# Graph layer with expert gates: gates kept in 32 partitions per tile of nodes, bias products of two tiles at a time, tiles in the order 0, 2, 1, 3

## The chip, the cores and the metric

One NeuronCore of a Trainium2 chip runs the whole program. The metric is the device time of one execution in microseconds, as the median of several runs. The engines are TensorE (PE in the rows, its weight loads PEld), VectorE (DVE), ScalarE (ACT), GpSimd (POOL) and SyncE (SP), which here only issues DMAs.

## What is computed

The reference is one layer over 12,500 nodes of 256 channels: a normalisation, a graph attention term and a linear attention term (phase 1 and the first half of phase 2 of the kernel), and then a feed-forward part with one shared and four gated expert networks. Only the last of these matters here:

```python
def _shared_mlp(x, W1, b1, W2, b2, W3, b3):
    h = jax.nn.relu(x @ W1 + b1)
    h = jax.nn.relu(h @ W2 + b2)
    return h @ W3 + b3
...
all_out = _experts_mlp(x, eW1, eb1, eW2, eb2, eW3, eb3)      # 4 experts, 256 -> 128 -> 64 -> 256
shared = _shared_mlp(x, sW1, sb1, sW2, sb2, sW3, sb3)         # 256 -> 256 -> 128 -> 256
gates = jax.nn.softmax(x @ gW + gb, axis=-1)
topv, topi = jax.lax.top_k(gates, TOPK)                       # the best 2 of 4
topw = jax.nn.softmax(topv, axis=-1)
sel = jnp.take_along_axis(all_out, topi[:, :, None, :], axis=-1)
gated = jnp.sum(sel * topw[:, :, None, :], axis=-1)
return shared + gated
```

Since the experts' last layer is linear, the kernel multiplies the hidden activations by the gates before the last weights, and adds the last biases as one more product: a row of up to 32 numbers for each node (its four gates as high part, low part and high part again, and two ones for the shared bias) times a matrix of 32 rows and 256 columns.

## The kernel before

The nodes are worked on in 25 groups of 500, a group being 4 tiles of 125 nodes (`T = 4`, `R = 125`). Phase 1 (to about 255 us) makes the tables that the graph term gathers from, and phase 2 (from about 255 us) is a software pipeline whose turn `i` does three stages: `a` for group `i`, `b` for group `i-1` and `c`, the feed-forward part, for group `i-2`. Turns 2 to 24 have all three stages, so there are 23 such turns; the groups 23 and 24 get their feed-forward part in `last_turn` and `end_turn`.

Each engine's instructions are written out by hand in program order, and engines wait for one another only by named semaphores. Nothing is reordered by a scheduler. The products are in fp32r, a rounded 32-bit form; one product with full accuracy is three of them (`split_mm`, L228 to L230: high by high, low by high, high by low).

The gates travel so. VectorE writes a group's gates into `scale_rows` (125 x 128: 32 numbers for each of the 4 tiles). TensorE transposes that (L606) into psum partitions 0 to 127, tile `j` in partitions 32j to 32j+31. ScalarE's `copy_scales` (L958 to L963) moves the four blocks of 32 partitions to `scaleT`, all of them to partitions 0 to 31, tile `j` in columns 125j to 125j+124. The other 96 partitions of `scaleT` and of `out_bias` hold zeros for good. `scaleT` is then read twice: by L691, which spreads the gates over the experts' channels with the selection matrix `gate_sel`, and at the end of the turn by L706, the bias product of each tile, `scaleT` (128 x 125) as weights and `out_bias` (128 x 256) streamed.

The last part of TensorE's turn is this, for each of the tiles 0, 1, 2, 3: one bias product, three products of the shared last layer, and six of the experts' last layer, all added up in one half of a psum bank (tiles 0 and 1 in bank 2, tiles 2 and 3 in bank 3). It waits for `e2_lo` (the low part of the gated activations, made by VectorE) ahead of tile 0's expert products. Its end is told by `out_mm`, for which VectorE's last addition of the turn waits. In `last_turn` and `end_turn` the same products stand in `out_shared` (bias and shared layer of four tiles, each tile in a bank of its own) and `out_experts`.

Two other places run TensorE in narrow form: `p2_den` (L507) and `logits_of_z` (L613) multiply 128 rows by only 32 columns of weights, four of them side by side, to psum partitions 0, 32, 64 and 96; they are plain fp32 products and show two records for each. `second_experts` (L595) does the same with 64 columns.

`small_constants` on VectorE builds `gate_sel`, `out_bias` and others once, near 234 to 240 us.

Of the kernel before, what the change touches and what calls it, by code (L numbers as in the profile page):

```python
# [8 lines left out]
ALU = mybir.AluOpType  # L9
ACT = mybir.ActivationFunctionType  # L10
# [3 lines left out]
C = 256  # L14
HEADS, HEAD_CH = 4, 64
MIX_HEADS, MIX_CH = 8, 32
EXPERTS, TOPK = 4, 2
LN_EPS, ATT_EPS = 1e-5, 1e-6

P = 128  # L20
R = 125
T = 4
# [7 lines left out]
QUAD = 32  # L30
# [6 lines left out]
for _name, _chunks, _cols in (("Wq", 2, 256), ("W1", 4, 512), ("W2", 4, 256), ("sW1", 2, 256), ("sW2", 2, 128),  # L37
# [2 lines left out]
    W_TOTAL += _chunks * _cols  # L40

SEMAPHORES = (
    "base", "den", "den_rows", "dx", "e1_mm", "e1_relu", "e2_hi", "e2_lo", "e2_mm", "e2_relu", "e2g",
    "g_hi", "g_split", "gate_rows", "gates", "gath0", "gath1", "gb", "gnn", "gw", "h_lo", "h_mm", "h_relu", "hb_mm", "ident", "lg", "lg_mm", "lt_mm",
    "idx0", "idx1", "k_exp", "kden", "k_hi", "k_mm", "k_split", "kf", "kvT", "kv_mm", "kx", "kxT", "kxs", "kxt_mm", "mT",
    "mT_hi", "m_mm", "m_norm", "masks", "mt", "mv_m", "mv_x1", "mv_y", "mv_z", "out", "out_mm", "p1_act",
# [9 lines left out]
def gps_layer(nc, A):  # L56

    ctx = ExitStack()
    with ctx:
# [5 lines left out]
        def due(count):  # L65

            return not isinstance(count, int) or count > 0
# [144 lines left out]
        def rowt(b, j):  # L212

            return psum[0:R, b + j // 2, (j % 2) * C:(j % 2 + 1) * C]
# [4 lines left out]
        def wslice(t, name, chunk, lo=0, n=None):  # L219
            at, cols = W_AT[name]  # L220
            at += chunk * cols + lo
            return t[:, at:at + (cols if n is None else n)]

        def split_mm(pe, out, w, x, first, last):


            (wh, wl), (xh, xl) = w, x
            pe.matmul(out, wh, xh, start=first, stop=False)  # L228
            pe.matmul(out, wh, xl, start=False, stop=False)  # L229
            return pe.matmul(out, wl, xh, start=False, stop=last)  # L230
# [195 lines left out]
        def _(pe):  # L426
# [11 lines left out]
            def tile(t, c, j):  # L438
                return t[:, c, j * R:(j + 1) * R]
# [134 lines left out]
            def w2_pair(i, pair, c):  # L574
# [12 lines left out]
                                        (wslice(w_hi, "W2", k), wslice(w_lo, "W2", k)), k == 0, k == 3)  # L587
                last.then_inc(S["w2"], 1)

            def second_experts(i, q):  # L590

                pe.wait_ge(S["e1_relu"], 4 * (i - 2) + 2 * q + 2)
                for m in range(2):
                    e = 2 * q + m
                    last = pe.matmul(psum[m * HEAD_CH:(m + 1) * HEAD_CH, 2 + q, 0:GR], second_w[:, e, :], e1[:, e, :],  # L595
                                     start=True, stop=True)
                last.then_inc(S["e2_mm"], 1)

            def phase2(i, par, a=True, b=True, c=True, own_q=True):
# [99 lines left out]
                if c:  # L699
                    if due(i - 1):  # L700
                        pe.wait_ge(S["s2_lo"], i - 1)
                    if due(2 * (i - 1)):
                        pe.wait_ge(S["e2_relu"], 2 * (i - 1))
                    for j in range(T):
                        out = rowt(2, j)
                        pe.matmul(out, scaleT[:, j * R:(j + 1) * R], out_bias[:], start=True, stop=False)  # L706
                        split_mm(pe, out, (s2_hi[:, j * R:(j + 1) * R], s2_lo[:, j * R:(j + 1) * R]),
                                 (wslice(w_hi, "sW3", 0), wslice(w_lo, "sW3", 0)), False, False)
                        if j == 0:
                            if due(i - 1):  # L710
                                pe.wait_ge(S["e2_lo"], i - 1)
                        for q in range(2):
                            last = split_mm(pe, out, (tile(h_hi, q, j), tile(h_lo, q, j)),
                                            (wslice(w_hi, "eW3", q), wslice(w_lo, "eW3", q)), False, q == 1)
                    last.then_inc(S["out_mm"], 1)

            def expert(e, bank):
# [32 lines left out]
            def out_shared(i, banks, lows):  # L750

                pe.wait_ge(S["t_s2"], lows)
                pe.wait_ge(S["e2_relu"], 2 * (i - 1))
                for j in range(T):
                    pe.matmul(psum[0:R, banks[j], 0:C], scaleT[:, j * R:(j + 1) * R], out_bias[:], start=True, stop=False)
                    split_mm(pe, psum[0:R, banks[j], 0:C], (s2_hi[:, j * R:(j + 1) * R], s2_lo[:, j * R:(j + 1) * R]),
                             (wslice(w_hi, "sW3", 0), wslice(w_lo, "sW3", 0)), False, False)

# [117 lines left out]
        def _(act):  # L876
# [81 lines left out]
            def copy_scales(i):  # L958
                if due(i - 1):
                    act.wait_ge(S["scale_t"], i - 1)  # L960
                for j in range(T):
                    last = act.activation(scaleT[0:QUAD, j * R:(j + 1) * R], psum[j * QUAD:(j + 1) * QUAD, 5, 0:R],  # L962
                                          ACT.Copy)  # L963
                last.then_inc(S["scaleT"], 1)

            def expert(i, e, bank):
# [201 lines left out]
        def _(dve):  # L1168
# [71 lines left out]
            def small_constants():  # L1240
                dve.memset(head_mask[:], 0.0)
                dve.drain()
                for h in range(P // MIX_CH):
                    dve.memset(head_mask[h * MIX_CH:(h + 1) * MIX_CH, h * MIX_CH:(h + 1) * MIX_CH], 1.0)
                dve.wait_ge(S["w_later"], 16 * LATER_LOADS)
                for e in range(EXPERTS):
                    hi, lo = PARTS[0] + e, PARTS[1] + e
                    tt(gate_sel[:, e // 2, e % 2 * HEAD_CH:(e % 2 + 1) * HEAD_CH],
                       ident[:, hi:hi + 1].broadcast_to([P, HEAD_CH]),
                       ident[:, lo:lo + 1].broadcast_to([P, HEAD_CH]), ALU.add)  # L1250
                dve.reduce_sum(low_rows[:, 0:QUAD], ident[:].rearrange("p (j r) -> p r j", r=QUAD), AXX)
                dve.reduce_sum(third[:], ident[:, PARTS[2]:PARTS[2] + 8], AXX)
                dve.tensor_copy(ob_hi[0:QUAD, :], ob_raw[0:QUAD, :])
                dve.wait_ge(S["zeroed"], 1)
                dve.tensor_copy(gate_w[:, :, 0:EXPERTS], gw_raw[:])
                dve.drain()
                ts(third[:], third[:], -1.0, None, ALU.mult)
                dve.reduce_sum(w2_nmean[:], w2, AXX)
                for q in range(CK):
                    at = [d + q * per for d in (0, MIX_HEADS)]  # L1260
                    tt(den_sel[:, q, :].rearrange("p (h n) -> p h n", h=per),
                       low_rows[:, at[0]:at[0] + per].unsqueeze(2).broadcast_to([P, per, MIX_CH]),
                       low_rows[:, at[1]:at[1] + per].unsqueeze(2).broadcast_to([P, per, MIX_CH]), ALU.add)
                dve.reduce_sum(low_rows[:, QUAD:QUAD + 1], low_rows[:, MIX_HEADS:2 * MIX_HEADS], AXX)
                dve.drain()
                ts(low_rows[:, QUAD:QUAD + 1], low_rows[:, QUAD:QUAD + 1], -1.0, None, ALU.mult)
                ts(w2_nmean[:], w2_nmean[:], -1.0 / C, None, ALU.mult).then_inc(S["w2_mean"], 1)
                stt(out_bias[0:QUAD, :], ob_hi[0:QUAD, :], third[0:QUAD, :], ob_raw[0:QUAD, :], ALU.mult, ALU.add)

            def second_parts(n):  # L1270

# [595 lines left out]
```

## Time and profile before

| | |
|---|---|
| median of 3 runs | 1368.28 us (1367.68 to 1369.21) |
| the profiled execution, its own time | 1367.16 us |
| its span, first to last instruction | 1365.4 us |
| TensorE busy | 1324.2 us, 97% of the span |
| VectorE, GpSimd, ScalarE busy | 1034.3, 826.1, 738.2 us |
| granted TensorE clock, mean | 0.995 |
| one turn of phase 2 | 43.0 us |

The span leaves out 1.8 us of the execution around it. A row of the timeline gives the start and length of an instruction, or of several alike. A matmul's length includes its passage through the array, so neighbours overlap: what one costs in a stream is the distance from its start to the next one's start.

### The profile page before, as it was taken

To read this page: it belongs to the slowest core of one execution; us is meant where nothing else is said; L and a number is where in the kernel's file an instruction comes from. 1 tells how busy PE (TensorE), PEld (TensorE's weight loads), DVE (VectorE), ACT (ScalarE), POOL (GpSimd) and SP (SyncE) were. 2 spreads that over 40 slices of the span, in tenths; PEclk is the share of its full clock that TensorE was granted. 3 is DMA by queue.
4 is the path that set the end of the run, shared out by engine and by line. 5 is a ranking of instruction groups with operands and counts; after the bars stand their busy time and mean duration, and the time that the engine had idled before them with its cause. 6 is when DMAs were issued, how large, how long until landed. Compare 5 with 4: busy or idle time off the path is not lost.

```text
span 1365.4 us, 26647 instructions
## 1 busy us (share of the span) xinstructions
PE 1324.2 (97%) x8932; PEld 1149.0 (84%) x8932; DVE 1034.3 (76%) x2615; ACT 738.2 (54%) x1339; POOL 826.1 (61%) x818
## 2 busy tenths in 40 slices
PE   5999999988999999999999999999999999999997
PEld 5999999876888888888888888888888888888886
DVE  6877677977787777877778777877778777787774
ACT  4555555334655655556554555545565455655554
POOL 4777676757555675556655666556665566655540
PEclk9999999999999999999999999999999999999999
DMA  5787767422211221112211222122221222211001
GB/s 172 253 267 244 241 209 254 130 60 68 63 39 54 76 75 46 52 55 76 72 41 58 57 76 71 29 70 58 76 68 31 68 61 76 68 31 60 17 16 31
DMA packets 71736, 121.81 MB, mean 89 GB/s; under 512 B 38034, under 2 KB 42767, under 8 KB 71704
## 3 DMA queue, kind: packets, MB, share of 16 engines
q1 hardware_dynamic: 55704, 108.00, 24.8%
q0 software_dynamic: 16000, 13.43, 4.5%
q8 instruction: 14, 0.23, 0.1%
q14 instruction: 18, 0.15, 0.0%
HBM read 69.47 MB, written 51.70 MB: 89 GB/s over the span
## 4 chain that ended last, share of the span: by engine, by line
PE 86%; DVE 5%; ACT 3%; issue 3%; POOL 2%; POOLq 1%; DMA 1%; DVEq 1%; SPq 0%; ACTq 0%
PE psum L228 26%; PE psum L229 25%; PE psum L230 25%; PE psum L434 5%; DVE qf L1473 2%; PE psum L691 1%; ACT s_hi L956 1%; PE psum L613 1%; PE psum L507 1%; PE psum L514 1%; ACT relu L955 1%; PE psum L706 1%; POOL xg L1753 1%; POOL ag L1755 1%; DMA attn_bc<-in_L_gnn_attn_l 0%
## 5 line engine op out<-in xcount | busy, mean ns | idle before, releaser
L1759 POOL TENSOR_TENSOR s_lo<-relu,s_hi 128x1000 fp32r<-128x1000 f32 (+1 forms) x47 | 85.4, 1816 | 148.9 <-ACT s_hi L956 143.4
L228 PE MATMUL psum<-w_hi,h_hi 128*125 128x256 f32 x600 | 171.1, 285 | 0.1
L229 PE MATMUL psum<-w_lo,h_hi 128*125 128x256 f32 x600 | 168.8, 281 | 0.0
L230 PE MATMUL psum<-w_hi,h_lo 128*125 128x256 f32 x600 | 168.6, 281 | 0.0
L1759 POOL TENSOR_TENSOR h_lo<-relu,h_hi 128x1000 fp32r<-128x1000 f32 x50 | 124.6, 2492 | 50.6 <-ACT h_hi L956 50.5
L1753 POOL DMA_INDIRECT xg<-table_xt,idx x100 | 124.9, 1249 | 39.5 <-issue 38.3
L1755 POOL DMA_INDIRECT ag<-table_al,idx x100 | 122.4, 1224 | 30.5 <-issue 30.5
L228 PE MATMUL psum<-z_hi,w_hi 128*128 128x500 f32 x300 | 121.5, 405 | 1.8 <-DVE z_lo L1543 1.0
L228 PE MATMUL psum<-xT_hi,w_hi 128*128 128x500 f32 x300 | 120.2, 401 | 0.0
L229 PE MATMUL psum<-xT_lo,w_hi 128*128 128x500 f32 x300 | 117.7, 392 | 0.0
L230 PE MATMUL psum<-xT_hi,w_lo 128*128 128x500 f32 x300 | 117.1, 390 | 0.0
L229 PE MATMUL psum<-z_lo,w_hi 128*128 128x500 f32 x300 | 116.7, 389 | 0.0
L230 PE MATMUL psum<-z_hi,w_lo 128*128 128x500 f32 x300 | 116.7, 389 | 0.0
L228 PEld LDWEIGHTS psum<-w_hi,h_hi 128*125 128x125 f32 x600 | 111.8, 186 | 5.1 <-issue 4.4
L880 ACT ACTIVATE row_n<-psum,nm_m,rs_m 125x256 f32<-125x256 f32 x100 | 48.2, 563 | 123.5 <-POOL nm_m L1696 123.5
L229 PEld LDWEIGHTS psum<-w_lo,h_hi 128*125 128x125 f32 x600 | 111.8, 186 | 0.0
L230 PEld LDWEIGHTS psum<-w_hi,h_lo 128*125 128x125 f32 x600 | 111.5, 186 | 0.0
L1415 DVE SCALAR_TENSOR_TENSOR base<-xb,rn,b_bc 125x256 f32<-125x256 f32 x100 | 93.7, 977 | 0.0
L962 ACT ACTIVATE scaleT<-psum 32x125 fp32r<-32x125 f32 x100 | 26.7, 267 | 120.5 <-PE psum L606 119.6
L1284 DVE TENSOR_SCALAR qf<-psum 128x1000 f32<-128x1000 f32 x25 | 30.0, 1199 | 78.2 <-PE psum L230 78.0
L1729 POOL TENSOR_TENSOR k_lo<-kf,k_hi 125x1024 fp32r<-125x1024 f32 x25 | 63.3, 2532 | 41.7 <-DVE k_hi L1227 41.7
L968 ACT ACTIVATE e<-psum,e_bias 128x500 f32<-128x500 f32 x100 | 65.0, 672 | 35.9 <-PE psum L230 35.9
(264 smaller groups left out, 4343.4 us busy)
## 6 DMA issues: line engine op xcount, KB each, us to landing
xb<-in_x SPq DMA_DIRECT2D x50, 448.0 KB
xT_hi_table<-x1T_hi SPq DMA_DIRECT2D x25, 500.0 KB
xT_lo_table<-x1T_lo SPq DMA_DIRECT2D x25, 500.0 KB
xT_hi<-xT_hi_table SPq DMA_DIRECT2D x25, 500.0 KB, 4.3
xT_lo<-xT_lo_table SPq DMA_DIRECT2D x25, 500.0 KB, 5.4
table_xt<-xts SPq DMA_DIRECT2D x25, 455.0 KB
out<-xmid SPq DMA_DIRECT2D x24, 448.0 KB
xb<-in_x SPq DMA_DIRECT2D x50, 52.0 KB
```

The lines of the kernel that those rows point to most:

```text
L228: pe.matmul(out, wh, xh, start=first, stop=False)
L229: pe.matmul(out, wh, xl, start=False, stop=False)
L230: return pe.matmul(out, wl, xh, start=False, stop=last)
L434: last = pe.transpose(psum[:, b + c, j * R:(j + 1) * R], src[:, j, c * P:(c + 1) * P], ident[0:R, 0:R])
L880: act.activation(out[:, j, :], src(j), ACT.Identity, bias=nm[which][:, j:j + 1], scale=rs[which][:, j:j + 1]).then_inc(S[done], 1)
L968: act.activation(e1[:, e, :], colT(bank), ACT.Relu, bias=e1_bias[:, e:e + 1]).then_inc(S["e1_relu"], 1)
L1284: ts(qf[:], colT(bank, 2), 0.0, None, ALU.min).then_inc(S["q_min"], 1)
L1415: last = stt(base[:, j, :], xb[par][:, j, :], rn2[par][:, 0, j:j + 1], b2_bc[:], ALU.mult, ALU.add)
L1729: ptt(k_lo[par][:], kf[par][:], k_hi[par][:], ALU.subtract).then_inc(S["k_split"], 1)
L1753: pool.indirect_dma_start(xg[par][:, j, :], None, table_xt.ap(), bass.IndirectOffsetOnAxis(idx[par][:, 1, j:j + 1], 0)).then_inc(S[f"gath{ ...
L1755: pool.indirect_dma_start(ag[par][:, j, :], None, table_al.ap(), bass.IndirectOffsetOnAxis(idx[par][:, 0, j:j + 1], 0)).then_inc(S[f"gath{ ...
L1759: ptt(out, src, hi, ALU.subtract).then_inc(S[done], 1)
```

## The change

The gates of tile `j` stay in partitions 32j to 32j+31 on their way into `scaleT`, which so becomes block-diagonal (zeros elsewhere, as before). `out_bias` gets four copies of its 32 rows, one for each block of partitions, by three more VectorE copies, and `gate_sel` picks a gate from any of the four blocks (`low_rows` is the identity folded over the four blocks). A bias product now reads only its tile's 32 rows of `scaleT` and of `out_bias`. In the turn the tiles go in two pairs, 0 and 2, then 1 and 3, so that the two bias products of a pair write two banks. In each pair come two bias products, six products of the shared layer and twelve of the experts' layer. The wait for `e2_lo` stands behind the first pair's shared products, and a new semaphore, `first_out`, is raised by the last of these and waited for ahead of the second pair's bias products; both are on TensorE. In `out_shared` the four bias products stand together ahead of the four tiles' shared products.

```diff
+            def bias_of_gates(out, j):
+
+                part = slice(j * QUAD, (j + 1) * QUAD)
+                pe.matmul(out, scaleT[part, j * R:(j + 1) * R], out_bias[part, :], start=True, stop=False)
...
-                    for j in range(T):
-                        out = rowt(2, j)
-                        pe.matmul(out, scaleT[:, j * R:(j + 1) * R], out_bias[:], start=True, stop=False)
-                        split_mm(pe, out, (s2_hi[:, j * R:(j + 1) * R], s2_lo[:, j * R:(j + 1) * R]),
-                                 (wslice(w_hi, "sW3", 0), wslice(w_lo, "sW3", 0)), False, False)
-                        if j == 0:
-                            if due(i - 1):
-                                pe.wait_ge(S["e2_lo"], i - 1)
-                        for q in range(2):
-                            last = split_mm(pe, out, (tile(h_hi, q, j), tile(h_lo, q, j)),
-                                            (wslice(w_hi, "eW3", q), wslice(w_lo, "eW3", q)), False, q == 1)
+                    for second in range(2):
+                        if second:
+                            pe.wait_ge(S["first_out"], i - 1)
+                        for j in (second, second + 2):
+                            bias_of_gates(rowt(2, j), j)
+                        for j in (second, second + 2):
+                            last = split_mm(pe, rowt(2, j), (s2_hi[:, j * R:(j + 1) * R], s2_lo[:, j * R:(j + 1) * R]),
+                                            (wslice(w_hi, "sW3", 0), wslice(w_lo, "sW3", 0)), False, False)
+                        if second == 0:
+                            last.then_inc(S["first_out"], 1)
+                            pe.wait_ge(S["e2_lo"], i - 1)
+                        for j in (second, second + 2):
+                            for q in range(2):
+                                last = split_mm(pe, rowt(2, j), (tile(h_hi, q, j), tile(h_lo, q, j)),
+                                                (wslice(w_hi, "eW3", q), wslice(w_lo, "eW3", q)), False, q == 1)
                     last.then_inc(S["out_mm"], 1)
...
                 for j in range(T):
-                    pe.matmul(psum[0:R, banks[j], 0:C], scaleT[:, j * R:(j + 1) * R], out_bias[:], start=True, stop=False)
+                    bias_of_gates(psum[0:R, banks[j], 0:C], j)
+                for j in range(T):
                     split_mm(pe, psum[0:R, banks[j], 0:C], (s2_hi[:, j * R:(j + 1) * R], s2_lo[:, j * R:(j + 1) * R]),
...
                 for j in range(T):
-                    last = act.activation(scaleT[0:QUAD, j * R:(j + 1) * R], psum[j * QUAD:(j + 1) * QUAD, 5, 0:R],
-                                          ACT.Copy)
+                    part = slice(j * QUAD, (j + 1) * QUAD)
+                    last = act.activation(scaleT[part, j * R:(j + 1) * R], psum[part, 5, 0:R], ACT.Copy)
...
+                for e in range(EXPERTS):
+                    hi, lo = PARTS[0] + e, PARTS[1] + e
+                    tt(gate_sel[:, e // 2, e % 2 * HEAD_CH:(e % 2 + 1) * HEAD_CH],
+                       low_rows[:, hi:hi + 1].broadcast_to([P, HEAD_CH]),
+                       low_rows[:, lo:lo + 1].broadcast_to([P, HEAD_CH]), ALU.add)
...
+                dve.drain()
+                for j in range(1, T):
+                    dve.tensor_copy(out_bias[j * QUAD:(j + 1) * QUAD, :], out_bias[0:QUAD, :])
```

On TensorE, at the end of a turn, the kernel before has this order (operands are named as the moving operand, then the weights: `out_bias,scaleT` is a bias product, `w,s` the shared layer, `w,h` the experts' layer):

```order
L706 MATMUL psum<-out_bias,scaleT 125x256 [waits s_e2_relu,s_s2_lo]
L228 MATMUL psum<-w_hi,s_hi 125x256
L229 MATMUL psum<-w_lo,s_hi 125x256
L230 MATMUL psum<-w_hi,s_lo 125x256
L228 MATMUL psum<-w_hi,h_hi 125x256 [waits s_e2_lo]
L229 MATMUL psum<-w_lo,h_hi 125x256
L230 MATMUL psum<-w_hi,h_lo 125x256
L228 MATMUL psum<-w_hi,h_hi 125x256
L229 MATMUL psum<-w_lo,h_hi 125x256
L230 MATMUL psum<-w_hi,h_lo 125x256
L706 MATMUL psum<-out_bias,scaleT 125x256
```

The changed kernel has at the same place, from the beginning of the first pair to the wait for `e2_lo`:

```order
L593 MATMUL psum<-out_bias,scaleT 125x256 [waits s_e2_relu,s_s2_lo]
L593 MATMUL psum<-out_bias,scaleT 125x256
L228 MATMUL psum<-w_hi,s_hi 125x256
L229 MATMUL psum<-w_lo,s_hi 125x256
L230 MATMUL psum<-w_hi,s_lo 125x256
L228 MATMUL psum<-w_hi,s_hi 125x256
L229 MATMUL psum<-w_lo,s_hi 125x256
L230 MATMUL psum<-w_hi,s_lo 125x256
L228 MATMUL psum<-w_hi,h_hi 125x256 [waits s_e2_lo]
```

The number of products is the same; bias products now stand in twos, and eight products rather than four stand ahead of the wait for `e2_lo`.

In `last_turn` on TensorE the bias products stood one ahead of each tile's three shared products:

```order
L755 MATMUL psum<-out_bias,scaleT 125x256 [waits s_e2_relu,s_t_s2]
L228 MATMUL psum<-w_hi,s_hi 125x256
L229 MATMUL psum<-w_lo,s_hi 125x256
L230 MATMUL psum<-w_hi,s_lo 125x256
L755 MATMUL psum<-out_bias,scaleT 125x256
```

Now the four stand together:

```order
L593 MATMUL psum<-out_bias,scaleT 125x256 [waits s_e2_relu,s_t_s2]
L593 MATMUL psum<-out_bias,scaleT 125x256 x3
L228 MATMUL psum<-w_hi,s_hi 125x256
L229 MATMUL psum<-w_lo,s_hi 125x256
L230 MATMUL psum<-w_hi,s_lo 125x256
```

Here too only the order and the rows that a bias product reads have changed.

## Rows read from the trace of the kernel before

**Rows 1.** The page: busy time and share of each engine; clock by slices.
```profile
PE 1324.2 (97%) x8932; PEld 1149.0 (84%) x8932; DVE 1034.3 (76%) x2615; ACT 738.2 (54%) x1339; POOL 826.1 (61%) x818
...
PEclk9999999999999999999999999999999999999999
```
**Rows 2.** The page: the chain that ended last, by engine.
```profile
PE 86%; DVE 5%; ACT 3%; issue 3%; POOL 2%; POOLq 1%; DMA 1%; DVEq 1%; SPq 0%; ACTq 0%
```
**Rows 3.** Two turns of phase 2: span, then busy us of PE, PEld, DVE, ACT, POOL, clock.
```profile
643.11:686.18 43.07, 42.89 (x278) 36.12 (x277) 33.20 (x90) 23.80 (x43) 26.29 (x25) 1.00 0.21 60
686.18:729.20 43.02, 42.85 (x277) 36.08 (x277) 33.05 (x90) 23.93 (x44) 26.38 (x25) 1.00 0.21 60
```
**Rows 4.** Waits of PE over the whole span: us in total, times, longest.
```profile
PE psum L691 <- ACT s_hi L956: 3.8, 22, 0.2
PE psum L434 <- ACT row_n L880: 2.6, 1, 2.6
PE psum L755 <- DVE s_lo L1539: 2.1, 1, 2.1
```
**Rows 5.** Timeline of PE and PEld at the end of a turn (start, length).
```profile
695.86 0.38 PE L230 MATMUL psum<-xT_hi,w_lo 128*128 128x500 f32 x1
695.86 0.18 PEld L706 LDWEIGHTS psum<-out_bias,scaleT 128*125 128x125 f32 x1
696.08 0.28 PE L706 MATMUL psum<-out_bias,scaleT 128*125 128x256 f32 x1
...
696.20 0.28 PE L228 MATMUL psum<-w_hi,s_hi 128*125 128x256 f32 x1
...
697.26 0.28 PE L706 MATMUL psum<-out_bias,scaleT 128*125 128x256 f32 x1
```
**Rows 6.** Groups by line: the bias products of turns 2 to 24.
```profile
L706 PE MATMUL psum<-out_bias,scaleT 128*125 128x256 f32 x92 | 26.0, 282 | 0.0
```
**Rows 7.** Timeline around L507: 128 rows by 32 columns, four side by side.
```profile
679.04 0.38 PE L229 MATMUL psum<-z_lo,w_hi 128*128 128x500 f32 x1
...
679.26 0.38 PE L230 MATMUL psum<-z_hi,w_lo 128*128 128x500 f32 x1
679.58 0.37 PEld L507 LDWEIGHTS psum<-qf,kden 128*32 128x32 f32 x16 [0.34 <-issue]
679.58 0.64 PE L507 MATMUL psum<-qf,kden 128*32 128x125 f32 x16
680.14 0.18 PEld L228 LDWEIGHTS psum<-w_hi,h_hi 128*125 128x125 f32 x1 [0.19 <-issue]
680.14 0.38 PE L228 MATMUL psum<-w_hi,h_hi 128*125 128x256 f32 x1
680.25 0.19 PEld L229 LDWEIGHTS psum<-w_lo,h_hi 128*125 128x125 f32 x1
680.36 0.28 PE L229 MATMUL psum<-w_lo,h_hi 128*125 128x256 f32 x1
```
**Rows 8.** The same L507, answers of narrower windows: first 4, 8, 12 records.
```profile
679.58 0.31 PE L507 MATMUL psum<-qf,kden 128*32 128x125 f32 x4
...
679.58 0.42 PE L507 MATMUL psum<-qf,kden 128*32 128x125 f32 x8
...
679.58 0.53 PE L507 MATMUL psum<-qf,kden 128*32 128x125 f32 x12
```
**Rows 9.** Waits of PEld ahead of L613 and L507: us, times, longest.
```profile
PEld psum L613 <- issue: 8.2, 23, 0.4
PEld psum L507 <- issue: 7.9, 23, 0.4
```
**Rows 10.** Timeline of DVE: constants at the end of phase 1.
```profile
237.16 0.27 DVE L1253 CAST ob_hi<-ob_raw 32x256 fp32r<-32x256 f32 x1
...
239.56 0.47 DVE L1268 SCALAR_TENSOR_TENSOR out_bias<-ob_hi,third,ob_raw 32x256 fp32r<-32x256 f32 x1
```
**Rows 11.** The copies of the gates on ACT, and how long ACT idled before them.
```profile
L962 ACT ACTIVATE scaleT<-psum 32x125 fp32r<-32x125 f32 x100 | 26.7, 267 | 120.5 <-PE psum L606 119.6
```

More of the change, by code:

```diff
@@ L42 @@
 SEMAPHORES = (
-    "base", "den", "den_rows", "dx", "e1_mm", "e1_relu", "e2_hi", "e2_lo", "e2_mm", "e2_relu", "e2g",
+    "base", "den", "den_rows", "dx", "e1_mm", "e1_relu", "e2_hi", "e2_lo", "e2_mm", "e2_relu", "e2g", "first_out",
     "g_hi", "g_split", "gate_rows", "gates", "gath0", "gath1", "gb", "gnn", "gw", "h_lo", "h_mm", "h_relu", "hb_mm", "ident", "lg", "lg_mm", "lt_mm",
@@ L1245, in small_constants @@
                 dve.wait_ge(S["w_later"], 16 * LATER_LOADS)
[L1246 to L1250, printed above, removed]
                 dve.reduce_sum(low_rows[:, 0:QUAD], ident[:].rearrange("p (j r) -> p r j", r=QUAD), AXX)
```

## The prediction, made before the changed kernel ran

> **What bounds the kernel now.** I read the page's busy shares first: TensorE is busy 97% of the span, at full granted clock (2.4 GHz) in every slice, and the next engine, VectorE, 76% [rows 1]. The chain that ended last agrees: 86% of it is TensorE [rows 2]. A turn of phase 2 takes 43.0 us, of which TensorE is busy 42.9, while VectorE has 33, GpSimd 26 and ScalarE 24 us of work [rows 3]. The waits say the same: the only one that comes back each turn is at L691, 3.8 us in 22 turns, 0.17 us each, and it ends a path that TensorE itself starts in the same turn [rows 4]. So inside phase 2 every nanosecond put on or taken off TensorE's stream shows in the time, one for one. A matmul's price in this stream is the distance between starts, not its listed length. At the end of a turn ten products of 256 columns go by from one bias product (696.08) to the next (697.26): 0.118 us each, weight load hidden (its record begins together with the matmul ahead of it) [rows 5]. A bias product is listed at 0.282 us [rows 6] but costs 0.118.
>
> **The change, part by part.**
>
> *What could be saved.* There are 92 bias products in the turns [rows 6], now in 46 pairs. A pair costs 2 x 0.118 = 0.236 us today.
>
> *How two narrow products run.* The trace has no product of 32 rows. It has the sister form, 128 rows by 32 columns, four side by side (L507), and that is the nearest row. Its records come in fours, and each further four lengthen the group by 0.11 us (0.31, 0.42, 0.53, then 0.64 for all 16) [rows 7, 8]. Four products at once so cost what one of them does; one record of fp32 with 125 columns takes two passes, 0.107 us. I take a pair of bias products as one stream of 256 columns at what two passes of 125 cost, 0.107 us; a slightly later start of the second would add at most 0.01.
>
> *What going into and out of the narrow form costs.* This is the term that decides. From the start of the last wide product ahead of L507 (679.26) to the start of L229 behind it (680.36) there are 1.10 us [rows 7]. In them lie the wide product's own 500 columns, 0.22 (679.04 to 679.26), four rounds of 0.107 = 0.43, and the 256 columns of L228, 0.12. Left over: 1.10 - 0.22 - 0.43 - 0.12 = 0.33 us, for one entry and one exit. I split it by the load records. The wide stream ends at 679.26 + 0.22 = 679.48, and the first narrow load begins at 679.58: 0.10 us in which nothing loads or streams. The last round ends at about 680.05, and the next wide load begins at 680.14: again 0.09. That load is now exposed: it begins at 680.14, the next load at 680.25, so 0.105 for 125 columns. The rest, 0.03, is the load of 32 columns on entry. The loads of L507 and L613 idle 0.35 us ahead of each group, 23 groups each, and the profile lays it to nothing that they wait for ("issue"), so it is no semaphore [rows 7, 9]. In the ordinary stream no such hole exists [rows 5].
>
> A pair of bias products between wide products then costs: 0.095 (stream before must end) + 0.105 (load of 125 columns, exposed; the other tile's load beside it) + 0.107 (both streams) + 0.095 + 0.105 (exit, load of the next wide product exposed) = 0.507 us. Against 0.236 before that is +0.27 us a pair, two pairs a turn +0.54, and 46 pairs x 0.27 = **+12.4 us**.
>
> The Trainium skill, "TensorEngine Tiling (Array Packing)", Key Properties, states that changing the tiling mode, and not just the tile, drains TensorE. The holes around L507 agree with it, but there the columns are cut and not the rows; that the row cut counts as such a mode as well is the page's statement (its Tiling Modes list both), and no run here shows it yet.
>
> *Last and end turn.* The four bias products there have a wait just ahead of them (2.1 us in one of the two [rows 4]), so entry is free. A group costs 0.105 + 0.107 + 0.02 + 0.095 + 0.105 = 0.43 instead of 0.105 + 4 x 0.118 = 0.58: -0.15 us, twice -0.3 at best, and 0 where the wait behind takes it up. I take -0.1.
>
> *The new wait and the order of tiles.* `first_out` is raised by TensorE itself, 12 expert products (12 x 0.118 = 1.4 us) ahead of where it is waited for; it costs 0. Queued behind it is only TensorE's own stream; if it stood open for the length of one matmul's passage (0.28), it would cost that. The wait for `e2_lo` moves from behind 4 products to behind 8: 0.5 us more cover for a wait that today shows no idle time [rows 5]. So nothing is gained there. `out_mm` still stands at the end of the turn. Bias, shared and expert products keep their number.
>
> *ScalarE.* Four copies of 32 x 125, 0.267 us each, as before, only to other partitions; ScalarE idles 120 us ahead of them in total [rows 11]. 0, and with 0.1 us more each they would still hide behind those waits and the products between them and L691.
>
> *VectorE's constants.* `gate_sel` from `low_rows` instead of `ident`: same size, 0. Three copies of 32 x 256 at 0.27 us (the cast of `ob_hi` [rows 10]) and a drain: about 0.9 us once, near 240 us, where TensorE does not wait for VectorE. 0, at worst +0.9.
>
> *Sum.* +12.4 - 0.1 = +12.3 us. The profiled execution takes 1367.16 (span 1365.4), so I expect 1379.5 of one like it; it lies 1.1 below the median of the runs, 1368.28, so the median should be **1380.6 us**.
>
> **Bounds of the price of a pair.** From below: no hole and no exposed load, both products in one stream: 0.125, that is -0.11 a pair, -5.1 us. From above: the two loads (0.105 each) follow one another and are not beside each other: +0.1 more a pair, +4.8 us on top, +17.1. I take the value next to the L507 rows, since entry, exit and side-by-side loads are all seen there.
>
> **The rivals.**
>
> *No stop between forms (not slower).* If cutting the rows needs no emptying of the array and loads stay hidden, a pair costs 0.118 + 0.007: 46 x 0.111 = -5.1, and the two groups of four save 0.33 each at most, -0.4 of it visible: -5.5, **1362.8 us**. For it: the two products are independent, in different rows and banks. Against: L507 and L613 lose 0.33 us at each visit with no wait. The case turns at a pair's price of 0.236: half of the lost 0.40 (two holes, two loads) would have to stay away for a gain.
> The Trainium skill, "TensorE: Matmul & The Clock Gate", Part 3 (Packing small matmuls), says that products in different groups of 32 rows run concurrently, four of them with 3.07 times the speed, and that weight loads go beside running matmuls where the row group differs. By that page alone the pair would be nearly halved in price. L507 agrees on the concurrency; the page gives no price for the change between forms.
>
> *Holes but hidden loads.* If the weights of the next form are loaded while the stream before still runs, a pair costs 0.095 + 0.107 + 0.095 = 0.297: +0.06 a pair, +2.7, **1371.0 us**. Against: in rows 7 the load visibly starts only after the hole.
>
> *The loads of the two tiles one behind the other.* +17.1, **1385.4 us**. L507's loads go side by side, but those are column strips.
>
> *The change does nothing.* 32 rows are run like 128, in the ordinary stream, 0.118 each: **1368.3 us**. Against: the 32-column form visibly is something else than the wide one.
>
> **How the numbers follow.** Chances: my forecast 0.58; loads in series 0.12; holes with hidden loads 0.09; nothing changes 0.05; no stop 0.16. The range reaches from the no-change case to just above the loads in series: 1368 to 1387, which leaves out the gain and tails on both sides, about 0.19. The likeliest case's own range is 1377 to 1384 (0.07 us a pair either way). A measurement of this kernel can tell about 0.2% (2.7 us) from no change. Faster by more: 0.16. Within: 0.05 and half of the case at +2.7, 0.10. Slower: 0.74.
>
> **What the profile after would show.** A turn of 43.0 + 0.54 = 43.6 us. PEld with an idle stretch laid to "issue" ahead of L593 and of the first L228 of the shared layer, twice a turn, as at L507 today. The two L593 matmuls of a pair starting within 0.01 us of each other, and about 0.51 us from the end of the wide stream before to the first shared product. Busy times of VectorE, ScalarE and GpSimd unchanged in a turn, no wait for `first_out`. I would be wrong if the two L593 records follow the stream before without a hole (then the gain), or start one 0.1 us or more behind the other (then the upper case); or if a turn that got longer on TensorE is caught up by a wait elsewhere, of which I see none but the 0.17 us at L691.

## The result and the profile after

The changed kernel takes 1380.6 us (median of 6 runs, 1379.7 to 1382.59) and the kernel before 1368.42 (6 runs, 1367.68 to 1369.21). The ratio is 1.009, 95% interval 1.0079 to 1.01: slower by 12.2 us, 0.9%. The profiled execution of the changed kernel is the slowest of its six, 1382.59 us (span 1380.8), and that of the kernel before took 1367.16 (span 1365.4), so the two profiles lie further apart than the medians.

The page of the changed kernel, busy time of each engine (answers to [rows 1]) and the chain that ended last ([rows 2]):

```profile
PE 1337.1 (97%) x8932; PEld 1145.8 (83%) x8932; DVE 1033.4 (75%) x2618; ACT 736.4 (53%) x1339; POOL 829.3 (60%) x818
...
PE 84%; DVE 6%; issue 3%; ACT 3%; POOL 2%; DVEq 1%; POOLq 1%; DMA 0%; SPq 0%; ACTq 0%
```

TensorE ran the same 8932 matmuls and is busy 13 us longer; no other engine grew by more than 3.2 us. (A busy PE is not a working PE: the holes found below count as busy, since a matmul's listed length, 0.38 us at 704.07, reaches beyond them.)

Two turns in the table of stretches (answers to [rows 3]; span, then busy time of PE, PEld, DVE, ACT and POOL):

```profile
650.86:694.39 43.53, 43.36 (x278) 35.93 (x277) 33.11 (x90) 23.73 (x43) 26.61 (x25) 1.00 0.21 60
694.39:737.90 43.51, 43.34 (x278) 35.93 (x277) 33.00 (x90) 23.79 (x44) 26.42 (x25) 1.00 0.21 60
```

A turn is half a microsecond longer. The steadiest measure of it is the spreading of the gates, which comes once a turn, 23 times. The first row is of the kernel before, the second of the changed one (first and last start of its 46 weight loads):

```profile
L691 PEld LDWEIGHTS psum<-scaleT,gate_sel x46: 186/188/190, 346.0 to 1292.1; 128*128 128x128 f32 x46
```
```profile
L696 PEld LDWEIGHTS psum<-scaleT,gate_sel x46: 186/188/190, 350.1 to 1307.3; 128*128 128x128 f32 x46
```

From turn 2 to turn 24 there are 22 turns: (1292.1 - 346.0 - 0.1) / 22 = 43.00 us before, (1307.3 - 350.1 - 0.1) / 22 = 43.50 after. (The last start is the second load of its group, 0.1 us behind the first.) The table under the experiments is made the same way.

Now the place itself. Timeline of PE and PEld of the changed kernel around both pairs of one turn (answers to [rows 5]):

```profile
703.85 0.38 PE L229 MATMUL psum<-xT_lo,w_hi 128*128 128x500 f32 x1
...
704.07 0.38 PE L230 MATMUL psum<-xT_hi,w_lo 128*128 128x500 f32 x1
704.38 0.18 PEld L593 LDWEIGHTS psum<-out_bias,scaleT 32*125 32x125 f32 x2 [0.34 <-issue]
704.39 0.38 PE L593 MATMUL psum<-out_bias,scaleT 32*125 32x256 f32 x2
704.69 0.18 PEld L228 LDWEIGHTS psum<-w_hi,s_hi 128*125 128x125 f32 x1
...
704.80 0.19 PEld L229 LDWEIGHTS psum<-w_lo,s_hi 128*125 128x125 f32 x1
704.92 0.28 PE L229 MATMUL psum<-w_lo,s_hi 128*125 128x256 f32 x1
...
706.83 0.29 PE L230 MATMUL psum<-w_hi,h_lo 128*125 128x256 f32 x1
707.04 0.18 PEld L593 LDWEIGHTS psum<-out_bias,scaleT 32*125 32x125 f32 x2
...
707.58 0.28 PE L229 MATMUL psum<-w_lo,s_hi 128*125 128x256 f32 x1
```

The two bias products are one entry of 0.38 us, which is what a single one takes in the four-trips run below; in the trace their starts are 3 to 4 ns apart, so they run side by side. The wide stream ahead ends at 704.07 + 0.22 = 704.29, and the first narrow load begins at 704.38: a hole of 0.09. From that load to the wide load of L228 there are 0.31 us (load, both streams, the next hole), and the next load after that begins 0.11 later (an exposed load). Worked out as for L507 in the prediction: from 704.07 to 704.92 are 0.85 us, less 0.22 for the wide product's 500 columns and 0.12 for L228's 256, leaves 0.51 for the pair. The second pair: 706.83 to 707.58 is 0.75, less 0.12 and 0.12, leaves 0.51. Before, two bias products cost 0.236. In the mean of the turns, the forty products of a turn's end (from the start of the wide product ahead to their last start) take 5.37 us, where the kernel before takes 4.87: the whole 0.50 of the turn lies here.

Of the signs that the prediction named, one is only half there: the first L593 load has its idle stretch laid to "issue", but ahead of L228 the loads pause for 0.13 us only (704.56 to 704.69), which the timeline does not mark. No wait for `first_out` shows.

### The profile page after: what moved, and what is told of

It reads as the page before. It is cut to its first block, busy times and chain, and to the rows that moved or that the text cites. A ratio compares the mean times of both kernels' runs of the same rounds, so it can differ in the third digit from the quotient of the medians.

```text
span 1380.8 us, 26651 instructions
## 1 busy us (share of the span) xinstructions
PE 1337.1 (97%) x8932; PEld 1145.8 (83%) x8932; DVE 1033.4 (75%) x2618; ACT 736.4 (53%) x1339; POOL 829.3 (60%) x818
## 4 chain that ended last, share of the span: by engine, by line
PE 84%; DVE 6%; issue 3%; ACT 3%; POOL 2%; DVEq 1%; POOLq 1%; DMA 0%; SPq 0%; ACTq 0%
PE psum L228 26%; PE psum L229 24%; PE psum L230 24%; PE psum L434 5%; DVE qf L1486 2%; PE psum L696 1%; ACT s_hi L966 1%; PE psum L593 1%; PE psum L618 1%; PE psum L507 1%; ACT relu L965 1%; PE psum L514 1%; POOL xg L1766 1%; POOL ag L1768 1%; DMA attn_bc<-in_L_gnn_attn_l 0%
## 5 line engine op out<-in xcount | busy, mean ns | idle before, releaser
L228 PE MATMUL psum<-w_hi,h_hi 128*125 128x256 f32 x600 | 170.7, 284 | 0.2
L228 PE MATMUL psum<-z_hi,w_hi 128*128 128x500 f32 x300 | 121.5, 405 | 1.8 <-DVE z_lo L1556 1.0
L228 PE MATMUL psum<-xT_hi,w_hi 128*128 128x500 f32 x300 | 121.0, 403 | 0.0
L228 PEld LDWEIGHTS psum<-w_hi,h_hi 128*125 128x125 f32 x600 | 111.5, 186 | 5.3 <-issue 4.4
L965 ACT ACTIVATE relu<-psum,h_bias 128x500 f32<-128x500 f32 x100 | 67.8, 678 | 31.0 <-PE psum L230 30.9
```

The costliest lines, as they stand in the source:

```text
L965: act.activation(out, colT(b), ACT.Relu, bias=bias)
```

## The experiments

Each row: the median and its ratio to the kernel before, run beside it on the same chip, with the 95% interval; and the turn, from the first and last start of the spreading of the gates in its profile.

| kernel | median, us | kernel before, us | ratio | turn, us |
|---|---|---|---|---|
| changed kernel | 1380.6 | 1368.42 | 1.009 (1.0079 to 1.01) | 43.50 |
| wide pairs | 1369.14 | 1368.94 | 1.0001 (0.9992 to 1.001) | 42.97 |
| layout only | 1370.24 | 1368.94 | 1.0007 (0.9998 to 1.0016) | 43.02 |
| same strip | 1387.02 | 1368.94 | 1.0132 (1.0116 to 1.0147) | 43.74 |
| one trip | 1372.64 | 1368.94 | 1.0028 (1.0018 to 1.0038) | 43.16 |
| four trips | 1402.98 | 1368.46 | 1.0251 (1.0237 to 1.0265) | 44.51 |
| 64 rows | 1380.33 | 1368.46 | 1.0083 (1.0069 to 1.0097) | 43.52 |
| narrow at the end | 1368.95 | 1368.46 | 1.0003 (0.9994 to 1.0012) | 43.01 |
| filled wait | 1363.92 | 1369.16 | 0.9965 (0.9951 to 0.9979) | 42.80 |
| order and fill | 1363.36 | 1369.16 | 0.9956 (0.9943 to 0.997) | 42.76 |

**Wide pairs: all of the change but the narrow products.**

```diff
-                pe.matmul(out, scaleT[part, j * R:(j + 1) * R], out_bias[part, :], start=True, stop=False)
+                pe.matmul(out, scaleT[:, j * R:(j + 1) * R], out_bias[:], start=True, stop=False)
```

> The changed kernel, with its order of tiles, its first_out wait and its block-diagonal gates, but each bias product reads all 128 rows (same sum, since the other blocks hold zeros). Theory (the price is that of going into and out of the 32-row form): the holes go away, a turn is 43.0 us again instead of 43.5, time 1368.4 to 1369.3 us, ratio to before 1.000 to 1.0007; no idle stretch ahead of the bias products. Rival (the new order of tiles, or the wait for first_out, costs): a turn stays near 43.5 us, time near 1380.

The time falls back to that of the kernel before, 0.2 us above it, within the interval. The wait for `first_out`, the new layout and the new order cost nothing that can be told from the scatter: the 12 us hang on this one line. The turn is even 0.03 us shorter than before (below).

**Layout only: the gates in four blocks, products and order of before.**

```diff
# against the wide pairs
-                    for second in range(2):
...
+                    for j in range(T):
+                        out = rowt(2, j)
+                        bias_of_gates(out, j)
```

> Only the layout of the change: gates in four blocks of partitions, out_bias copied to four blocks, gate_sel from low_rows; the products read 128 rows and stand in the order of before. Theory: turns of 43.0 us, 0 to +0.9 us from VectorE's longer constants, 1368.4 to 1369.3 us. Rival (the layout costs more: gate copies slow to other partitions, or constants late on the path to phase 2): 1370 or more, and turn 2 starting later than 341.9 us.

A turn costs the same as before (43.02 against 43.00). The time is a miss: the median is 1.3 us above the kernel before (ratio 1.0007) and lies where the rival put it, at 1370 or more. The interval still takes in no difference, and goes up to 2 us; wide pairs, with the same constants, is 0.2 us above. VectorE's constants in the profile of the changed kernel (start, length) answer to [rows 10]:

```profile
238.93 0.62 DVE L1266 TENSOR_TENSOR gate_sel<-low_rows 128x64 fp32r<-128x64 f32 x4
...
240.25 0.47 DVE L1278 SCALAR_TENSOR_TENSOR out_bias<-ob_hi,third,ob_raw 32x256 fp32r<-32x256 f32 x1
240.78 0.88 DVE L1281 CAST out_bias<-out_bias 32x256 fp32r<-32x256 f32 x3
```

The three copies take the 0.9 us that were foreseen. Whether they reach the end of the program is not settled. The first spreading of the gates begins at 347.9 us in the profile of layout only and at 346.0 before, but between 347.2 and 348.2 in three kernels further down that have the constants of before. The granted clock of the head of phase 2 goes with it. On the page, the tenth slice of the changed kernel (310.7 to 345.2 us) shows an 8 where the kernel before has a 9 [rows 1]:

```profile
PEclk9999999998999999999999999999999999999999
```

From 255 to 345 us the mean granted clock is 0.94 before (first spreading at 346.0); 0.92 in wide pairs, layout only, four trips, filled wait and order and fill (347.2 to 348.2, with either constants); and 0.91 in the changed kernel (350.1) and the four others (347.9 to 349.0). Here TensorE still waits a good deal (before, it is busy for 76 of these 90 us). Ahead of the first spreading, the stretches at the lower of the clock's two levels (granted 0.50, 1.2 GHz) are 10.2 us long together in the kernel before and 17.1 in the changed one. So most of the difference between the heads of these profiles goes with the clock, and at an equal 0.92 the longer constants don't show.

**Same strip: both products of a pair in one strip of rows.** The biases of tiles 2 and 3 are left out of the sum in the turns.

```diff
-                part = slice(j * QUAD, (j + 1) * QUAD)
+                strip = j % 2 if out_strips == 1 else j
+                part = slice(strip * QUAD, (strip + 1) * QUAD)
```

> The changed kernel, but both bias products of a pair in the turns read the same strip of 32 rows (that of tile 0 for 0 and 2, that of tile 1 for 1 and 3), so the biases of tiles 2 and 3 are left out of the sum. Same number of trips into the 32-row form. Theory (the two strips did run side by side): each pair gets longer by one stream of 256 columns, 0.107 us, 46 times, +4.9 us on the changed kernel: 1385.5 us, turn 43.7. Rival (they did not): no difference, 1380.6.

The timeline of PE and PEld at the first pair of a turn:

```profile
748.04 0.39 PE L230 MATMUL psum<-xT_hi,w_lo 128*128 128x500 f32 x1
748.36 0.29 PEld L594 LDWEIGHTS psum<-out_bias,scaleT 32*125 32x125 f32 x2 [0.35 <-issue]
748.36 0.49 PE L594 MATMUL psum<-out_bias,scaleT 32*125 32x256 f32 x2
748.78 0.18 PEld L228 LDWEIGHTS psum<-w_hi,s_hi 128*125 128x125 f32 x1
...
749.01 0.28 PE L229 MATMUL psum<-w_lo,s_hi 128*125 128x256 f32 x1
```

The pair's entry grows from 0.38 to 0.49 us and its loads from 0.18 to 0.29: the second load and stream stand behind the first. By the same subtraction the pair costs 749.01 - 748.04 - 0.22 - 0.12 = 0.63 us. The turn grows by 43.74 - 43.50 = 0.24, 0.12 a pair. The time is 18.1 us above the kernel before, 5.9 more than the changed kernel's 12.2; 4.9 were expected. The stream behind another costs the full 0.12 step and not 0.107, which gives 5.5; the rest is within the scatter. So in the change the two strips did run side by side, loads and streams both.

**One trip: all four bias products of a turn behind one entry.** (The edit in part.)

```diff
-                part = slice(j * QUAD, (j + 1) * QUAD)
...
+                part = slice(j // 2 * 2 * QUAD, (j // 2 * 2 + 1) * QUAD)
...
-                    for second in range(2):
...
+                    for j in (0, 2, 1, 3):
+                        bias_of_gates(rowt(2, j), j, j % 2 == 0)
+                    for j in range(T):
+                        out = rowt(2, j)
...
-                    last = act.activation(scaleT[part, j * R:(j + 1) * R], psum[part, 5, 0:R], ACT.Copy)
+                    to = slice(j // 2 * 2 * QUAD, (j // 2 * 2 + 1) * QUAD)
+                    last = act.activation(scaleT[to, j * R:(j + 1) * R], psum[j * QUAD:(j + 1) * QUAD, 5, 0:R], ACT.Copy)
```

Tiles 0 and 1 share a strip (and a psum bank), tiles 2 and 3 another. Only the first bias product of each bank carries `start=True`.

> All four bias products of a turn in one trip into the 32-row form: gates of tiles 0 and 1 in one strip, of 2 and 3 in another, order 0, 2, 1, 3, then shared and expert products tile by tile as before. Theory (a trip costs about 0.38 us whatever stands in it): one trip 0.38 + 2 x 0.107 = 0.60 us against 4 x 0.118 = 0.47, +0.12 us a turn, 1371 to 1372 us. Rival (the price hangs on each narrow product, 0.126 us for each of 92): as the changed kernel, 1380. Rival (pair and wait order): as the changed kernel without the order, 1368.4.

```profile
742.83 0.39 PE L230 MATMUL psum<-xT_hi,w_lo 128*128 128x500 f32 x1
743.15 0.29 PEld L593 LDWEIGHTS psum<-out_bias,scaleT 32*125 32x125 f32 x4 [0.36 <-issue]
743.15 0.49 PE L593 MATMUL psum<-out_bias,scaleT 32*125 32x256 f32 x4
743.58 0.18 PEld L228 LDWEIGHTS psum<-w_hi,s_hi 128*125 128x125 f32 x1
...
743.80 0.28 PE L229 MATMUL psum<-w_lo,s_hi 128*125 128x256 f32 x1
```

In the timeline of the same place, four products take what two in one strip take: 743.80 - 742.83 - 0.22 - 0.12 = 0.63 us, where 0.60 were forecast. The turn is 43.16, 0.14 above the layout alone, and the time 3.7 us above the kernel before (1372.64, just over the 1371 to 1372 expected): with half the trips, most of the loss is gone, with the same 92 narrow products. That rules out a price for each product. It is still slower than the wide form: 0.63 against 0.47.

**Four trips: the kernel before, and each bias product alone in the narrow form.**

```diff
-                        pe.matmul(out, scaleT[:, j * R:(j + 1) * R], out_bias[:], start=True, stop=False)
+                        pe.matmul(out, scaleT[0:QUAD, j * R:(j + 1) * R], out_bias[0:QUAD, :], start=True, stop=False)
```

> The kernel before with one edit: the bias product of a turn reads only partitions 0 to 31 of scaleT and out_bias (the others hold zeros, same sum), so each of the four stands alone in the 32-row form between wide products; nothing else of the change. Theory (a trip costs about 0.38 us beside its stream): 0.38 + 0.107 - 0.118 = +0.37 us for each of 92 products, +1.48 us a turn (44.5 us), +34 us, 1402.5 us. Rival (price per narrow product, 0.126 each as in the changed kernel): 1380. Rival (only two strips working side by side cost): 1368.4.

```profile
754.12 0.39 PE L230 MATMUL psum<-xT_hi,w_lo 128*128 128x500 f32 x1
754.44 0.18 PEld L706 LDWEIGHTS psum<-out_bias,scaleT 32*125 32x125 f32 x1 [0.35 <-issue]
754.45 0.38 PE L706 MATMUL psum<-out_bias,scaleT 32*125 32x256 f32 x1
754.75 0.18 PEld L228 LDWEIGHTS psum<-w_hi,s_hi 128*125 128x125 f32 x1
...
754.98 0.28 PE L229 MATMUL psum<-w_lo,s_hi 128*125 128x256 f32 x1
```

One product alone shows the same rows as a pair: hole, load, 0.38, wide load 0.31 behind the narrow one, and it costs 754.98 - 754.12 - 0.22 - 0.12 = 0.52 us by these rounded times (0.50 in the mean of the turns). The turn is 1.51 us longer, 0.38 for each trip, and the time 34.5 us, against 34 expected. A product of 32 rows is thus not cheaper than one of 128, and is dearer by 0.38 us when it stands alone. This is one edited line, with nothing else of the change, and it is the strongest of the tests: the number of trips was doubled against the change, and the cost came out where it should.

**64 rows in place of 32.**

```diff
-                part = slice(j * QUAD, (j + 1) * QUAD)
+                part = slice(j // 2 * 2 * QUAD, (j // 2 + 1) * 2 * QUAD)
```

> The changed kernel with bias products of 64 rows: tiles 0 and 1 read partitions 0 to 63, tiles 2 and 3 partitions 64 to 127 (zeros in the other block, same sum). Theory (the price is that of the change of form, not of the number of rows): as the changed kernel, 1380.6 us, turn 43.5, within 0.5 us. Rival (a hole or load that grows or shrinks with the rows): apart by 0.05 us a pair or more, 2.3 us.

```profile
746.66 0.39 PE L230 MATMUL psum<-xT_hi,w_lo 128*128 128x500 f32 x1
746.98 0.38 PE L593 MATMUL psum<-out_bias,scaleT 64*125 64x256 f32 x2
...
747.51 0.28 PE L229 MATMUL psum<-w_lo,s_hi 128*125 128x256 f32 x1
```

A pair costs 747.51 - 746.66 - 0.22 - 0.12 = 0.51 us again. The time is 11.9 us above the kernel before, where the changed kernel had 12.2, and the turn 43.52. Products of 64 rows cost as those of 32 do.

**Narrow at the end.** Against the changed kernel, with the order of before in the turns:

```diff
+                        pe.matmul(out, scaleT[:, j * R:(j + 1) * R], out_bias[:], start=True, stop=False)
```

> Narrow bias products only in the last and the end turn (four side by side, four banks, behind a wait); in the 23 turns they read all 128 rows in the order of before. Theory: 0.1 to 0.3 us less than the layout alone, so 1368.2 to 1369.0 us, not told apart from before by the time; in the profile the stretch from the first of the four to the first shared product is about 0.33 us. Rival (entry costs 0.1 even behind a wait, or four strips load one after another): 0.4 us or more there.

The time can't tell it from the kernel before. The timeline of the end turn:

```profile
1358.70 0.22 PEld L593 LDWEIGHTS psum<-out_bias,scaleT 32*125 32x125 f32 x4 [1.03 <-issue]
1358.73 0.39 PE L593 MATMUL psum<-out_bias,scaleT 32*125 32x256 f32 x4 [0.64 <-ACT relu L1077]
1359.05 0.18 PEld L228 LDWEIGHTS psum<-w_hi,s_hi 128*125 128x125 f32 x1
...
1360.82 0.18 PEld L228 LDWEIGHTS psum<-w_hi,h_hi 128*125 128x125 f32 x1 [0.28 <-DVE h_lo L1543]
```

From the first narrow load to the wide one are 0.35 us for four products side by side, 0.33 foreseen. With the exposed wide load behind it that is 0.46, against 0.105 + 4 x 0.118 = 0.58 for four wide ones behind the same wait: by this sum the narrow form is 0.12 us cheaper here. But nothing comes of it. The experts' products behind the shared layer wait for `h_lo` from VectorE, and that wait is 0.28 us long here where it is 0.17 in the kernel before:

```profile
1358.87 0.18 PEld L228 LDWEIGHTS psum<-w_hi,h_hi 128*125 128x125 f32 x1 [0.17 <-DVE h_lo L1534]
```

(The four of the last turn run at a mean granted clock of 0.66 and can't be compared.)

**Filled wait.** If every hole on TensorE counts one for one, closing one must gain. The kernel before has one at the exit from the 64-column form, where it waits for the shared activations at L691. Three products of the message stage are ready there, and were moved ahead:

```diff
+            def p2_m_begin(i):
+                pe.wait_ge(S["qz"], i + 1)
+                for q in range(1):
+                    split_mm(pe, rowt(6, 0), (tile(z_hi, q, 0), tile(z_lo, q, 0)),
+                             (g_hi[:, q, :], g_lo[:, q, :]), q == 0, q == CK - 1)
...
                        second_experts(i, q)
+                    p2_m_begin(i)
                     if due(i - 1):
                         pe.wait_ge(S["scaleT"], i - 1)
```

> The kernel before, with the first three products of the message stage (tile 0, first half) moved from behind to ahead of the spreading of the gates (L691), to where TensorE leaves the 64-column form of the experts' second layer and waits for the shared activations. Theory (a hole on TensorE counts one for one, and it can be filled with work that is ready): the load ahead comes about 0.2 us earlier, the 0.17 us of waiting for ScalarE go, a turn 42.8 us, 4 to 5 us less in 23 turns, 1363.5 to 1365 us. Rival (the gates arrive later and VectorE's product with them or the chain behind it takes the gain back): a turn of 43.0, 1368.4 us.

In the kernel before (first fence, PE and PEld) the load of L691 comes at 646.96 behind 1.01 us without a load, and its product behind 0.18 us without a stream; with the wait filled (second fence) the three products stand there and the spreading follows with no idle time:

```profile
646.96 0.30 PEld L691 LDWEIGHTS psum<-scaleT,gate_sel 128*128 128x128 f32 x2 [1.01 <-issue]
646.99 0.69 PE L691 MATMUL psum<-scaleT,gate_sel 128*128 128x500 f32 x2 [0.18 <-ACT s_hi L956]
```
```profile
689.32 0.18 PEld L228 LDWEIGHTS psum<-g_hi,z_hi 128*125 128x125 f32 x1 [0.79 <-DVE z_lo L1483]
...
689.66 0.31 PEld L698 LDWEIGHTS psum<-scaleT,gate_sel 128*128 128x128 f32 x2
689.78 0.62 PE L698 MATMUL psum<-scaleT,gate_sel 128*128 128x500 f32 x2
```

(`z_lo`, which the profile names there, was ready at 688.87; the load came at 689.32.) The turn is 42.80, 0.20 shorter, which makes 4.6 us in 23 turns, and the time is 5.2 us below the kernel before, a ratio of 0.9965. The later gates took nothing back.

**Order and fill.** The same, with the order 0, 2, 1, 3 and wide bias products at the end of the turn:

```diff
-                    for j in range(T):
-                        out = rowt(2, j)
-                        pe.matmul(out, scaleT[:, j * R:(j + 1) * R], out_bias[:], start=True, stop=False)
...
+                    for pair in ((0, 2), (1, 3)):
+                        for j in pair:
+                            pe.matmul(rowt(2, j), scaleT[:, j * R:(j + 1) * R], out_bias[:], start=True, stop=False)
```

> The same, and the end of a turn in the order of the change (pairs 0, 2 and 1, 3) with bias products that read 128 rows and the gate layout of before. Theory: the order alone gave 0.03 us a turn in the trace of the wide pairs, so 0.6 us less than the filled wait alone, 1363 to 1364.5 us, not told apart from it by the time. Rival: no difference or more.

1363.36 us, 5.8 below the kernel before on that chip and the best here; the 0.6 us from the order are within what the runs scatter, but the turn is 42.76 against 42.80, as it is 42.97 for the wide pairs against 43.02 for the layout alone. Part of both differences is scatter: three kernels with the old order and no narrow product in their turns have 43.00, 43.01 and 43.02. The forty products themselves, from the start of the wide product ahead to the last start, take 4.866 to 4.867 us in the mean of the 23 turns in four kernels with the old order (before, layout only, narrow at the end, filled wait), 4.843 in wide pairs and 4.836 here. So the order gives 0.02 to 0.03 us a turn.

## Why the prediction was right

The median was forecast at 1380.6 and measured at 1380.6. The agreement to the tenth is luck: the turns came out 0.9 us below the forecast, 0.7 us that no run explains made up for it, and the interval of the ratio alone is 1.4 us wide either way. The mechanism and the price of a pair are what the runs bear out.

- *A TensorE nanosecond counts one for one.* Shown in both directions: +1.51 us a turn (34.7 in 23 turns) gave +34.5 us in the time, -0.20 a turn (-4.6) gave -5.2.
- *The price of a trip, from the rows of L507.* 0.507 us was forecast for a pair and 0.51 is read in both pairs. The holes (0.09), the exposed loads (0.11) and the two products side by side are all there in the rows. That the column form stood in well for the row form was the assumption; the four-trips run, with nothing else changed, shows the price of the row form by itself: a trip with one product costs 0.38 us more than the wide product that it replaces.
- *The rule of the Trainium skill* ("TensorEngine Tiling (Array Packing)", Key Properties) that a change of tiling mode drains TensorE: the traces agree, for rows as for columns, with about 0.09 us without load or stream each way and the next weight load uncovered. The rule for the rival ("TensorE: Matmul & The Clock Gate", Part 3), that products in different groups of rows run concurrently, held too: two strips cost 0.51 and two products in one strip 0.63. The page's 3.07 is for four products in four strips, and it says nothing of the way in and out; no run here has four strips in one of the 23 turns, and four products in two strips, in one trip, cost 0.63 against 0.47.
- *The turns.* +0.54 a turn forecast, +0.50 measured, so 11.5 us in 23 turns and not 12.4. Of the missing 0.04, 0.02 to 0.03 is the new order of tiles, which the prediction put at nothing; the rest is within what the turns scatter. Why the order helps wasn't tested.
- *Last and end turn.* -0.1 forecast. The end turn's group is 0.12 us cheaper and the wait for `h_lo` behind it 0.11 longer, so 0 there, the case that the prediction had named ("0 where the wait behind takes it up"). From the last spreading's load to the end of the span are 1365.4 - 1292.1 = 73.3 us before and 1380.8 - 1307.3 = 73.5 after, with 0.50 more for turn 24 in it. The 0.3 that this leaves can't be laid to the narrow products: the same stretch is 72.5 us in layout only and 73.4 in wide pairs, which have none.
- *The constants.* 0 forecast, +0.9 at worst. The turns leave 12.2 - 11.5 = 0.7 us of the measured difference, 1.0 with the 0.3 above. The constants could be it (layout only was 1.3 us higher, wide pairs 0.2), but so could the clock: of the 25 runs of the kernel before that stand beside wide pairs, the ten with a granted clock of 0.992 took 1369.6 us in the mean and the seven with 0.995 took 1368.1, and four of the six runs of the changed kernel have 0.992. It is also within the interval. So this rest stays open.
- *The clock.* "At full granted clock in every slice" reads more out of the page than it says: a 9 stands for 90% or more. The kernel before has 10.2 us at the lower level near 280 and 311 us (the granted clock from 310 to 320 us is 0.66), all ahead of the turns that the sum is about. From 345 to 1330 us it is 1.00, so the sum isn't touched.
- *Where the case turns.* The prediction says that half of the lost 0.40 would have to stay away for a gain. By its own terms it is 0.507 - 0.236 = 0.27, two thirds. Nothing else was worked out from it.
- *The new wait, ScalarE's copies, the wait for `e2_lo`:* nothing, as forecast; wide pairs has all of them and no longer turn.
- Of the rivals, no stop between forms, holes with hidden loads, and no change at all are excluded by the rows; loads in series too (the pair's load entry is 0.18 long, and 0.29 where they do follow one another).

## What to carry to other kernels

Price a narrow product by the trip, not by the product: look in the trace for any narrow group that the kernel already has, subtract the streams from the distance between the wide products around it, and what is left is the toll for going in and out. Here, with 125-column weights, a narrow product alone costs 0.38 us more than a wide one, as much as three products of 256 columns. Packing two products that cost 0.118 each can't repay it. Four in four strips are 0.12 us cheaper where a wait covers the entry, and here the next wait took that up. And where an engine bounds the kernel, look for holes behind its waits and narrow groups and put ready work there: moving three products was worth 5 us, more than any form of the packing.

## What the hardware showed that I had not expected

- The toll is the same for 32 and for 64 rows (0.51 us a pair), and for one product and for two: what is paid is the change of form, and it made no difference here which of the two forms it was.
- The order of the wide products at the end of a turn, tiles 0, 2, 1, 3 in place of 0, 1, 2, 3, makes the forty products there 0.02 to 0.03 us shorter in sum (4.87 to 4.84), with the same products and no idle time for a wait on either side.
- The head of the program, up to turn 2, moves by some us between profiled executions: the first spreading of the gates began at 346.0 and 347.5 us in two kernels that share all the code ahead of it, and at 347.2 and 348.2 in two that have but three products moved ahead of it. The earliest has a granted clock of 0.94 from 255 to 345 us, the others 0.92. A single profile can't settle a microsecond there without a look at the clock.
